# A GNN kernel's node pass: its 392 row-map transfers handed out to the rounds in another proportion

## The reference, cut to what matters

```python
h = maximum(layernorm(x), 0); x = x + L0_gat_x5(h, edges)     # five attention layers
h = maximum(layernorm(x), 0); x = x + L1_hgt(h, edges)        # typed attention
h = maximum(layernorm(x), 0); x = x + L2_gcn(h, edges)        # gelu of normalized sums
h = maximum(layernorm(x), 0); x = x + L3_typed_gat(h, edges)  # typed attention, confounders
```

## Time and profile before

| | us |
|---|---|
| median of 3 runs (5265.82 to 5279.68) | 5274.59 |
| the profiled execution, its own time | 5282.94 |
| its span | 5281.2 |
| PE busy / DVE busy / ACT busy / POOL busy in the span | 4279.7 / 3999.5 / 3330.9 / 3275.7 |
| first power of the node pass starts | 109.4 |
| power of round 132 starts | 1522.0 |

### The profile page before, as it was taken

One profiled execution on the slowest core, in us unless ns is written; L12 is line 12 of the kernel. 1 busy time (PEld: TensorE's weight loads), 2 busy tenths in 40 slices (PEclk: granted clock), 3 DMA queues, 4 the chain that ended last, 5 costly groups with the idle time before them and its releaser, 6 DMA issues. The chain is left out here.

```text
span 5281.2 us, 101919 instructions
## 1 busy us (share of the span) xinstructions
PE 4279.7 (81%) x28013; PEld 3705.1 (70%) x28013; DVE 3999.5 (76%) x15157; ACT 3330.9 (63%) x9065; POOL 3275.7 (62%) x2905
## 2 busy tenths in 40 slices
PE   4889999999976978969969958776985858879575
PEld 4777777778866867858858847644775847757475
DVE  5789888889986767767767767687676959859765
ACT  2777777777755866847847847643873537758400
POOL 2878888887777727637457367222761257566277
PEclk6999999999988989979989979955997979989755
DMA  2999987666645636636636546487773659857332
GB/s 91 180 219 221 222 220 216 214 215 208 209 164 125 144 85 134 135 77 142 128 91 142 109 107 143 108 251 224 168 154 93 192 143 247 238 112 131 74 94 85
DMA packets 1107280, 825.56 MB, mean 156 GB/s; under 512 B 209510, under 2 KB 1068202, under 8 KB 1106396
## 3 DMA queue, kind: packets, MB, share of 16 engines
q1 hardware_dynamic: 1026800, 690.47, 50.4%
q0 software_dynamic: 77040, 128.08, 12.6%
q10 hardware_dynamic: 2880, 0.50, 0.1%
HBM read 374.78 MB, written 448.11 MB: 156 GB/s over the span
## 5 line engine op out<-in xcount | busy, mean ns | idle before, releaser
L806 POOL DMA_INDIRECT gat_G<-table,k_src_row x980 | 1073.2, 1095 | 316.5 <-issue 285.6
L1599 ACT ACTIVATE gat_Gw<-gat_G,gat_al 128x128 f32<-128x128 f32 x1960 | 618.6, 395 | 89.2 <-DVE gat_al L1424 89.2
L1455 DVE SCALAR_TENSOR_TENSOR gat_Gw<-gat_own,gat_al,gat_Gw 128x128 f32<-128x128 f32 x1960 | 554.1, 342 | 68.0 <-ACT gat_Gw L1599 67.8
L1716 PE MATMUL gat_psG<-gat_ends_at,gat_Gw 128*128 128x128 f32 x3920 | 538.1, 282 | 43.4 <-DVE gat_Gw L1455 43.3
L1744 PE MATMUL gat_psZ<-gat_aggT,t_gat_wh 128*128 128x256 f32 x1960 | 525.3, 391 | 12.0 <-ACT gat_hT L1625 11.6
L1716 PEld LDWEIGHTS gat_psG<-gat_ends_at,gat_Gw 128*128 128x128 f32 x3920 | 493.2, 197 | 54.6 <-DVE gat_Gw L1455 51.6
L635 PEld LDWEIGHTS nodes_psR<-t_ident_v,nodes_hTl 128*128 128x128 f32 x3168 | 433.2, 192 | 106.0 <-issue 1.7
L635 PE MATMUL nodes_psR<-t_ident_v,nodes_hTl 128*128 128x132 f32 x3168 | 448.3, 278 | 0.0
L479 POOL TENSOR_TENSOR nodes_rstd<-nodes_var,k_half 128x14 f32<-128x14 f32 x140 | 375.0, 2678 | 96.5 <-DVE nodes_var L546 96.5
L1625 ACT ACTIVATE gat_hT<-gat_psZ,t_gat_bias 128x256 f32<-128x256 f32 x490 | 231.6, 473 | 264.4 <-PE gat_psZ L1745 261.0
L1744 PEld LDWEIGHTS gat_psZ<-gat_aggT,t_gat_wh 128*128 128x128 f32 x1960 | 339.2, 193 | 53.3 <-ACT gat_aggT L1606 14.0
(11 more groups left out here) (668 smaller groups left out, 12726.0 us busy)
## 6 DMA issues: line engine op xcount, KB each, us to landing
table<-nodes_rows SPq DMA_DIRECT2D x660, 198.0 KB
table<-nodes_n SPq DMA_DIRECT2D x396, 192.0 KB
gat_own<-table SPq DMA_DIRECT2D x490, 132.0 KB
table<-gat_rows SPq DMA_DIRECT2D x392, 132.0 KB
nodes_x<-in_x SPq DMA_DIRECT2D x132, 192.0 KB
out<-nodes_x_out SPq DMA_DIRECT2D x132, 192.0 KB
gat_G<-table,k_src_row POOLq DMA_INDIRECT x980
hgt_q<-enter_q SPq DMA_DIRECT2D x98, 144.0 KB
```

The lines of the kernel that those rows point to most:

```text
L806: eng.indirect_dma_start(to, None, table, bass.IndirectOffsetOnAxis(ap=index, axis=0)).then_inc(sem, 16)
L1455: ins = eng.scalar_tensor_tensor(Gw[:, i % RS, t, h, :], own[:, i % RO, t, 0:D], al[:, g % 2, 1, a:a + 1], Gw[:, i % RS, t, h, :], ALU.mul ...
L1599: ins = eng.activation(Gw[:, i % RS, t, h, :], G[:, i % RG, t, 0:D], ACT.Copy, scale=al[:, g % 2, 0, a:a + 1])
L1716: mm = eng.matmul(o[:, h * P:(h + 1) * P], Gw[:, i % RS, t, h, :], ends_at[:, i % RE, t, :], start=True, stop=True)
```

## The change

The list of 392 steps stays as it is, and so does its order. How many of it a round takes is now read from a table `upto`, made when the kernel is built: round k takes the steps from `upto[k]` to `upto[k+1]`. The first NS = 98 rounds take 239 steps, evenly, which is 2 or 3 a round; the 34 rounds from 98 to 131 take the other 153, alternately 4 and 5. The first got falls into round 80 in place of round 65, the last into round 131 in place of round 130.

```diff
                 steps = [("put", c) for c in range(C)] + [("got", c) for c in range(C)] 
-                per = (len(steps) + N - 1) // N
+                first_rounds = 239
+                upto = [first_rounds * k // NS if k <= NS else
+                        min(first_rounds + (len(steps) - first_rounds) * (k - NS) // (N - NS), len(steps)) for k in range(LAST + 2)]
                 gather_slots(0)
                 gather_slots(1)
                 for k in range(LAST + 1):
...
-                    for what, c in steps[k * per:(k + 1) * per]:
+                    for what, c in steps[upto[k]:upto[k + 1]]:
```

## The result

| | before | changed |
|---|---|---|
| median of 8 runs each, us | 5277.73 | 5293.42 |
| range, us | 5265.82 to 5293.88 | 5289.18 to 5305.28 |
| profiled execution, us | 5282.94 | 5299.64 |

The ratio is 1.0034, 95% interval 1.0025 to 1.0043: slower by 13 to 23 us. Both intervals lie above 1, and both hold the 0.3% from which a difference was to count, so that it is slower is shown, that it is so by more than 0.3% is not. The forecast was 5288 us, 13 over before, with 0.5 on less than 0.3% and 0.4 on slower; the time lies in its range and the sum has the right direction.

A forecast was written before the change was run, and what follows sets the result against it. In the node pass it took POOL and DMA to bound rounds 0 to 10, then DMA, a PE-ACT loop, POOL, and PE without slots. Terms -9 + 0 - 4 - 6 + 32 = +13 us on 5274.6 gave 5288 us, range 5260 to 5311.

The forecast's parts named there:

- Part 5: Rounds 98 to 131, without slots: 153 gots (gathers) instead of 98 make POOL last; +32 us, bounds 0 and +36.
- it is self-consistent (once POOL is last, DVE starts from the power's end and the collision recurs): Late rounds: DVE's additions keep delaying a gather, 2.04 us in place of 0.95; round 10.57 us, +32 us.
- The upper bound of +36: Late rounds: the most they could lose, with POOL's power at 2.90 us in every round.
- Part 1: Rounds 65 to 95: 76 transfers instead of 93; round falls from 11.28 us to the PE-ACT loop's 10.97; -9 us.
- Part 2: Rounds 24 to 64: 100 transfers instead of 123; nobody waits for POOL, so 0 us, bounds 0 and -34.
- The sign I had named for it: Rounds 24 to 64: the DMA share was to fall to about 0.9.
- Part 3: Rounds 0 to 10: 26 puts (row-map writes) instead of 33, slot gathers also awaited; -4 us, bounds 0 and -10.
- Part 4: Rounds 11 to 23, taken as DMA-bound: 32 puts (row-map writes) instead of 39; -6 us, bounds 0 and -10.5.
- a fifth fewer puts take about 0.06 off a share of 1.10: Rounds 11 to 23: fewer row-map writes lower the DMA load, which was taken as the bound; -6 us.
- the first (no collision): Late rounds: DVE's additions don't delay gathers, so they cost 0 to +8.5 us; total 5256 to 5264 us, chance 0.16.
- the second (nothing gained early): Rounds 0 to 23: slot gathers and the pass's own stores set them, no gain; total 5298 to 5302 us, chance 0.18.
- the third (nothing moves): POOL sets neither the 11.28 us rounds nor the last 34; total 5275 us, chance 0.08.

The follow-up runs named there:

- e8: Changed kernel with POOL's bias addition cut to 16 of 384 columns from block 98 on; ratio to before 0.9978, rounds 98 to 131 took 326.5 us.
- e9: Changed kernel with DVE's three two-SBUF-input additions cut to 16 of 384 columns from round 98; ratio to before 0.9994, rounds 98 to 131 took 330.7 us.
- e1: Changed kernel, but slot rounds keep before's three transfers; late rounds get 153 gots (gathers), 55 of them repeats; ratio to before 1.0034, 5287.56 us.
- e7: Changed kernel with no row-map transfers in rounds 0 to 23, all 239 in rounds 24 to 97; 5306.93 us in one run.
- e11: Changed kernel with the split moved to 222 transfers in slot rounds and 170 after, 5 in each late round; 5301.41 us in one run.
- e4: The changed kernel again, unedited, in a second comparison with before; ratio 1.0026, late rounds 349.3 us.
- e10: Changed kernel with the split moved to 256 transfers in slot rounds and 136 after, 4 in each late round; ratio to before 1.0011.
- e3: Changed kernel with the split moved to 273 transfers in slot rounds and 119 after, 3.5 a late round; ratio to before 0.9991.
- e12: The split of 273 transfers in slot rounds and 119 after, against the changed kernel's 239 and 153, run once more; ratio to before 0.9982.
- e2: Changed kernel with the last 55 gots (gathers) left out, so 98 remain in late rounds; ratio to before 0.9991, 5262.66 us.

## Why the prediction was right, and where its terms were off

- *Part 5, +32, measured +22.6.* The mechanism held in the main: the loss is made between POOL's and DVE's lists and not by PE or the DMA (e8), and DVE's additions hold up a got (e9). It held by half in that POOL is last in the 5-got rounds only. The term was mis-sized in its step "it is self-consistent (once POOL is last, DVE starts from the power's end and the collision recurs)", which took 1.09 us as the loss of every such got. With 4 and 5 in turn each second round puts DVE last again, and the got after it then loses 0.59 us; in the other rounds, after DVE has waited for the power, the collision does recur at the same 0.25 us after the first addition, and costs 0.17. That isn't a matter of 4 or 5 gots alone: e1 has 18 late gots of 2.0 us or more, e7 with the changed kernel's late list 9, e11 with five in every round 12, the changed kernel 2 and e4 1. Forecast were 9.94 and 11.19 us for the two kinds of round; measured are 9.74 and 10.41. In the other direction there was a cost that I hadn't counted: POOL's bias addition holding a small DVE instruction, 1.3 us in the 4-got round. And 5.4 and 4.0 us in the two profiles are the pause in round 121, which nothing in the earlier trace rows shows. Without it the term is some +18. The upper bound of +36 doesn't follow from its reason: the 11.19 us that it starts from already hold a power of 2.90.
- *The Trainium skill's rule.* "SBUF — State Buffer", section "Who interferes with whom", infers that a tensor_tensor on DVE doesn't stall the making of DMA descriptors. By e9's fall from 1051 to 970 ns and e11's 2.04 us got the measurement decides against it for an indirect DMA. The same section's other sentence, that a DVE instruction with two SBUF inputs contends with a GpSimd instruction that reads SBUF, fits, if the got's reading of its indices is such a read; no run separates the two.
- *Part 1, -9, measured -6 in the mean.* The floor of 10.97 us was right to 0.2% (339.4 / 31 = 10.95). The step that failed is the one before it: I took 11.28 us as what three gots a round cost, from one execution. It is one of the paces of the same kernel, and the change gains 10 us against the one and nothing against the other.
- *Part 2, 0, measured +1.0.* Right: 449 to 451 us in all profiles with 2.3 to 3 a round, so POOL's list doesn't set these rounds; that the PE-ACT loop does is read from the waits of the earlier trace rows and no run tests it. The sign I had named for it, a DMA share of 0.9, was wrong: it is 0.98. The share isn't proportional to the puts in flight; e7 shows only that without any it is 0.67.
- *Part 3, -4, measured -2.8*; with no puts at all it is about -4 (e7: 110.3). Since e10 (109.0) and e11 (109.2) are as low with 28 and 24 puts there, the puts don't set the floor; that the slot gathers do, as the part supposed, isn't tested.
- *Part 4, -6, measured -0.1.* The failed step is "a fifth fewer puts take about 0.06 off a share of 1.10" as a gain in time: a share over 1 was read as the bound. e4 has 1.06 and runs at the PE-ACT loop's pace.
- *The sum.* +13 against +14.5 in the pass: the late term was 9 us too large, the early terms 10 us too good. That they cancelled is luck. The rivals: the first (no collision) would have needed the late rounds at 9.82 or under, and they take 10.3 in the mean; the second (nothing gained early) named rounds 0 to 23 nearly rightly, but put the late term at +32 to +36; the third (nothing moves) is out, by both intervals and the late stage's +22.6.

## What to carry to other kernels

Filling an engine up to its average slack costs nothing only as far as its instructions keep their durations. Here 1.6 us of slack took half a got of 1.25 for nothing, the next half cost 10 us over 34 rounds. Two instructions can meet at the same place in every round and still cost 0.17 us in one execution and 1.09 in another. Before a term is built on one stretch of one profile, ask what in it depends on where two engines stand to each other: such a stretch can have two paces, or change over in the middle, and a second execution shows it for little. A DMA share over 1 is a load, not yet a wait; look for who waits.

## What the runs showed of the hardware

- POOL's issue of an indirect DMA and DVE's additions with two SBUF inputs meet so that the issue gets longer: 0.95 us becomes 1.12, 1.28, 1.54, 2.04 or 2.28. It ends some 0.82 us after the end of one of the three additions, of the third in most (start plus 2.28 at 0.02 us into them in e8, 2.04 at 0.26, 1.54 at 0.77, 1.28 at 1.03), of the first in those of 1.12 us; from a start 0.25 to 0.28 us into them both 1.12 and 2.04 occur. With the additions narrowed the mean is 0.97. For the other direction, a DVE instruction of 0.19 us with two SBUF inputs took 1.49 us beside POOL's 1.01 us addition.
- POOL paused 3.2 to 6.2 us before one indirect DMA in rounds 119 to 127, after 104 to 106 gots of the late rounds, in nine profiles of kernels with more than three gots in late rounds (the changed kernel twice, e1, e3, e8 to e12), but not in e7, which has as many of them, nor in the four with three (before's three, e2). Its cause wasn't tried.
- The 4-byte puts raise the DMA share from 0.67 to 1.06 at the same 221 GB/s without moving the time.
